# Attention beside a scan and eight experts on one core: values of four score rounds in one step, turned scores first in a round, four exponential buffers

## The reference

```
xn    = layernorm(x)
u     = conv4(xn @ W_in + b_in)               # causal, per channel, 512 channels
h_t   = tanh(A) h_{t-1} + u_t Bp ; y_t = Cp h_t + Dp u_t      # 16 states, 512 steps
out1  = silu(y) @ W_out + b_out
q,k,v = xn @ W_qkv + b_qkv                    # 16 heads of 16
out2  = softmax(q k^T / 4) v
gate  = softmax(xn @ W_gate + b_gate), the best 2 of 8 kept
out3  = sum_e gate_e (xn @ W_experts[e] + b_experts[e])
out   = x + out1 + out2 + out3
```

## Time and profile before

| | |
|---|---|
| median of three runs | 803.84 us |
| the profiled execution itself | 803.87 us |
| its span, first to last instruction | 802.1 us |
| PE busy | 769.0 us (96%) |
| DVE busy | 586.1 us (73%) |
| ACT busy | 535.7 us (67%) |
| POOL busy | 392.5 us (49%) |
| exponentials | 256, 1.03 us each |
| mean granted TensorE clock | 0.992 |

### The profile page before, as it was taken

The page is one execution under the profiler, slowest core; times in us unless marked ns, Lnnn a source line. Parts: engine busy times, 40 slices in busy tenths (PEclk is TensorE's granted clock), DMA queues, the critical chain, the costliest instruction groups (busy, mean ns, idle before and its releaser), DMA issues.

```text
span 802.1 us, 13231 instructions
## 1 busy us (share of the span) xinstructions
PE 769.0 (96%) x4404; PEld 449.3 (56%) x4404; DVE 586.1 (73%) x845; ACT 535.7 (67%) x926; POOL 392.5 (49%) x527
## 2 busy tenths in 40 slices
PE   9789999999999999999999999999999998999996
PEld 7556565665556555565555655555555554554553
DVE  6789966977588676896679775887758877578720
ACT  4647766676676676776667766767666766667774
POOL 7644653574364534563436733355243552425554
PEclk9889999999999999999999999999999999999999
DMA  8302111031110311112111321103111211212000
GB/s 272 66 2 65 44 28 38 18 93 40 41 41 6 90 41 41 41 38 71 40 33 36 83 52 41 41 6 90 40 42 40 54 49 24 52 42 64 19 2 26
DMA packets 32465, 39.09 MB, mean 49 GB/s; under 512 B 8513, under 2 KB 18535, under 8 KB 32398
## 3 DMA queue, kind: packets, MB, share of 16 engines
q1 hardware_dynamic: 31418, 37.29, 17.8%
q10 hardware_dynamic: 852, 0.80, 0.3%
q0 software_dynamic: 128, 0.16, 0.1%
HBM read 8.74 MB, written 4.19 MB: 16 GB/s over the span
## 4 chain that ended last, share of the span: by engine, by line
PE 75%; DVE 18%; issue 4%; ACT 2%; SPq 0%; DMA 0%; POOL 0%; POOLq 0%; DVEq 0%; ACTq 0%
PE PS L456 38%; PE SB L583 12%; DVE mx L1041 10%; PE PS L616 9%; PE TB L600 5%; PE PS L513 4%; DVE ys L891 2%; PE PS L472 2%; PE PS L623 1%; DVE xn L1017 1%; DVE xl L923 1%; PE PS L547 1%; DVE ys L887 1%; PE PS L468 1%; PE PS L526 1%
## 5 line engine op out<-in xcount | busy, mean ns | idle before, releaser
L1041 DVE TENSOR_REDUCE mx<-SB 128x2 f32<-128x1024 f32 x256 | 313.0, 1223 | 153.9 <-PE SB L583 152.9
L1104 POOL TENSOR_TENSOR acc<-acc,mt 128x256 f32<-128x256 f32 x320 | 250.5, 789 | 255.4 <-ACT mt L668 190.0
L823 ACT ACTIVATE Pt<-TB 128x1024 f32<-128x1024 f32 x251 | 257.4, 1026 | 44.0 <-PE TB L600 41.2
L668 ACT ACTIVATE mt<-PS,cpad 128x256 f32<-128x256 f32 x256 | 107.4, 471 | 85.8 <-PE PS L456 85.4
L583 PE MATMUL SB<-kst,qst 48*128 48x512 f32 x512 | 128.6, 499 | 14.9 <-DVE mx L1041 11.5
L616 PE MATMUL PS<-Pt,V 128*17 128x512 f32 x1024 | 134.7, 598 | 1.1 <-ACT Pt L823 1.1
L583 PEld LDWEIGHTS SB<-kst,qst 48*128 48x128 f32 x512 | 47.8, 184 | 117.6 <-DVE mx L1041 63.4
L456 PE MATMUL PS<-weh,xTh 128*128 128x512 f32 x256 | 110.3, 431 | 2.1 <-DVE xl L923 1.1
L600 PE MATMUL TB<-qst,kst 50*128 50x512 f32 x502 | 101.3, 398 | 0.4 <-ACT Pt L823 0.2
L456 PE MATMUL PS<-wel,xTh 128*128 128x512 f32 x256 | 101.3, 396 | 0.0
L456 PE MATMUL PS<-weh,xTl 128*128 128x512 f32 x256 | 100.7, 393 | 0.0
(11 more groups left out here) (162 smaller groups left out, 1158.7 us busy)
## 6 DMA issues: line engine op xcount, KB each, us to landing
qst<-qkh SPq DMA_DIRECT2D x124, 64.0 KB, 2.3
kst<-qkh SPq DMA_DIRECT2D x124, 64.0 KB, 2.3
out<-acc SPq DMA_DIRECT2D x8, 512.0 KB, 2.8
qst<-qkl SPq DMA_DIRECT2D x62, 64.0 KB, 2.2
kst<-qkl SPq DMA_DIRECT2D x62, 64.0 KB, 2.3
acc<-in_x SPq DMA_DIRECT2D x7, 512.0 KB, 3.8
Bt<-in_wexp SPq DMA_DIRECT2D x2, 512.0 KB, 7.9
raw<-in_wexp SPq DMA_DIRECT2D x2, 512.0 KB, 9.6
```

The source lines that it names most:

```text
L668: return e.activation(mt[:, item % NM, :], P, ACT.Copy, scale=scale)
L823: e.activation(Pt[:, T % NP, :, :], turned_bank(T)[:, :, :], ACT.Exp, scale=0.25).then_inc(s_ex, 1)
L1041: e.tensor_reduce(mx[:, g % 2, 0:2, 4 * jj + a], SB[:, :, :], AX.X, ALU.max).then_inc(s_mx, 1)
L1104: e.tensor_tensor(v, v, mt[:, item % NM, :], ALU.add).then_inc(s_mt, 1)
```

## The change

1. `NP = 4`: a fourth buffer of exponentials (4 KB per partition). The DMA scratch of the program is set to 8192 to make room.
2. `values_at(t)`: values are issued in every fourth round, for the exponentials of four rounds at once: in round LAG + 3 + 4m, `values(2m)` and `values(2m+1)`. The second of them reads the exponential of the very round in which it stands.
3. In each round `turned` is written ahead of `score`.
4. The planner puts no unit into a round with values, no Z into the round ahead of one, and has other costs (0.43 for a pair of scores, 0.8 for each values).
5. Four of the eight start-up DMAs go from POOL's queue to ACT's.

```diff
-NP = 3
+NP = 4
...
+def values_at(t):
+
+    m, rest = divmod(t - LAG - 3, 4)
+    return (2 * m, 2 * m + 1) if rest == 0 and 0 <= m < STEPS // 4 else ()
...
-        return 0.45 * pairs + 1.05 * (LAG + 2 <= t < STEPS + LAG + 2 and (t - LAG) % 2 == 0)
+        return 0.43 * pairs + 0.8 * len(values_at(t))
...
-        spent = min(spent, 1.0) + max(left / max(last - t, 1), vector[t]) - fixed(t) - sum(COST[u[0]] for u in row)
+        share = left / max(last - t, 1)
+        spent = min(spent, 1.0) + share + 0.7 * max(vector[t] - share, 0.0) - fixed(t) - sum(COST[u[0]] for u in row)
...
-        while True:
-            k = next((k for k, u in enumerate(todo) if soonest(*u) <= t), None)
-            if k is None or spent < COST[todo[k][0]] / 2 - 0.8 * bare or len(row) > 2 and todo[k][0] != "B":
+        while not values_at(t):
+            k = next((k for k, u in enumerate(todo) if soonest(*u) <= t and not (u[0] == "Z" and values_at(t + 1))), None)
+            if k is None or spent < COST[todo[k][0]] / 2 - 1.2 * bare or len(row) > 2 and todo[k][0] != "B":
...
+                if LAG <= t < STEPS + LAG:
+                    turned(t - LAG)
                 if 0 <= t < STEPS:
                     score(t)
-                if LAG <= t < STEPS + LAG:
-                    turned(t - LAG)
-                m, odd = divmod(t - LAG - 2, 2)
-                if odd == 0 and 0 <= m < STEPS // 2:
+                for m in values_at(t):
                     values(m)
...
-                    else:
+                    elif T < 3:
                         e.wait_ge(s_lo[(W_Q0, W_VG, W_IN)[T]], 1)
...
+                        e.wait_ge(s_kp, 3)
+                        for k in range(4, 8):
+                            shifted_rows(e, k, s_rr[1])
...
-            e.wait_ge(s_kp, 3)
-            for k in range(4, 8):
-                shifted_rows(e, k, s_rr[1])
...
-    nc = _bacc.Bacc("TRN2", target_bir_lowering=False, num_devices=1)
+    nc = _bacc.Bacc("TRN2", target_bir_lowering=False, num_devices=1, dynamic_dma_scratch_size=8192)
```

## The result

The changed kernel takes **841.94 us** (median of 4 runs, 841.14 to 843.75) against 804.07 of the kernel before beside it (803.81 to 805.48): a ratio of 1.047, 95% interval 1.0448 to 1.0492. It is slower by 38 us, where 2.4 us less were forecast; the range ended at 808.5. The profiled execution has a span of 839.3 us, 37.2 more than before.

The account below looks back on a forecast made before the run. PE's own order was taken to bound the kernel (busy 96% of the span), with DVE stopping it in places. Terms -9.9 - 11.9 + 18.4 + 1.0 = -2.4 us took 803.87 to 801.4 us, range 795 to 808.5.

Parts of the forecast that it names:

- Fewer changes of form: On PE, values entered 64 times instead of 128, whole-array work 201 instead of 215: 9.9 us less.
- DVE's stop behind values: Scores right behind values no longer wait on PE for DVE's maximum: 11.9 us less.
- The new wait inside the values: Second values wait on PE for their own round's exponential, 0.37 us behind an M unit: 18.4 us more.
- ACT becomes the bound: Rival: exponentials late in values rounds behind tanh, roundings or copies in ACT's queue, costing 7.6 instead of 1.0: 808; chance 0.18.
- Turned scores first: Turned scores, 0.33 us earlier in their round, sometimes wait on PE for the exponential before: 1.0 us more.
- Start-up DMAs: Four issues moved to ACT cost nothing: PE's 2.67 us idle before the first Z covers 2.69; without cover 2.7 more.
- The fixed rest: Everything else in the kernel: same units, copies and DMAs, larger tile and smaller scratch without an instruction; no time added.
- DVE's lateness moves: Rival: DVE's irregular 4.2 us at scores stay, the later score adds up to 1: about 805; chance 0.12.

Follow-up runs that it names:

- e1: The changed kernel with values one round later and five exponential buffers, the planner following: 800.94 us, ratio 0.9964 to the kernel before.
- e7: e1 with ACT's copy of the values' bank and the unit P that reads it one round later too: 794.83 us, ratio 0.9883.
- e5: The changed kernel with ACT doing the exponential ahead of the previous round's closing unit in values rounds: 824.28 us, ratio 1.0251.
- e2: The changed kernel with score ahead of turned scores in each round again: 840.44 us, ratio 1.0451.
- e4: The kernel before with turned scores ahead of the score in each round, nothing else: 808.60 us, ratio 1.0060.
- e11: The kernel before with the four start-up DMA issues on ACT's queue, nothing else: 806.95 us, ratio 1.0029.
- e6: The changed kernel with a planner that puts at most one Q unit into a round, from round 8 on: 835.60 us, ratio 1.0397.
- e10: The changed kernel with LAG = 12, all one round later in the cycle of eight, the second values' wait kept: 818.41 us, ratio 1.0172.
- e12: e7 with four exponential buffers instead of five: 816.61 us, ratio 1.0148.

## Why the prediction was wrong

Step by step, as the prediction had them:

- *Fewer changes of form*, 9.9 us: right. The ledger has 10.7. Two values follow at 0.87 us, where 0.88 was taken, and not at 0.98: three pairs of the changed kernel and 63 of e1 show it. The rule of the Trainium skill (TensorE: Matmul & The Clock Gate, Part 3, "What overlaps and what doesn't") that weight loads run ahead only onto other rows of the array did not hold here; e1's and e7's pairs show it.
- *DVE's stop behind values*, 11.9 us: right; 11.2 gone.
- *The new wait inside the values*, 18.4 us: the mechanism and its unit price were right (0.83 and 1.91 us against 0.84 and 1.92). The size was low by about 6: eight of 64 pairs are 8.4 us above the price, seven of them since the exponential stood in ACT's queue behind a tanh, most often a late one, and the rest is within 2 us of it. This is what the rival "ACT becomes the bound" had in mind, but it looked for the cost at the turned scores, and it came at the second values. e5 shows what putting the wait right is worth: 17.7 us.
- *Turned scores first*, 1.0 us: right. By the ledger turned scores wait 1.8 us for exponentials in the change and 0.5 before, and e2 took only 1.5 us off by undoing it, which isn't clear of the noise. Alone on the kernel before it costs 4.5 to 5 (e4).
- *Start-up DMAs*, 0: wrong, with the cover misread. PE's 2.67 us of standing before the first Z was the same chain that the issues lengthen, not slack beside it. 2.1 to 2.3 us in e11, within the bound of 2.7. The changed kernel's own trace shows the same 2.1: from SP's first issue to the first Z it takes 14.12 us (25.16 to 39.28) where it took 12.00 (26.04 to 38.04). Its first turned scores are only 0.2 us later than before, since its start-up came to the issues 0.9 us sooner and the rounds behind the first Z took 1.1 us less.
- ***The fixed rest, "the same units, copies and DMAs"*: the step that failed.** The units are the same, but the planner put them in other rounds, and I priced their work and not their waits. 23 us of waits for banks, and 6.5 more in matmuls at the halved clock, whose stretches begin at such waits or right behind them (one at a wait for an exponential), make most of what the prediction lacks; the prediction had no term for the clock. Another 1 to 2 us went to weights not loaded ahead. I had read the order at three places, two around values and one in the start-up. The places that cost most lie at rounds 72 and 104, where the plan's rows read Q, Q and then X, T, T, and at 40, 136 and 168, where they are nearly so. The line of the plan, DVE's five pieces of work between two maxima, and three banks would have shown it: before, the values round 103 with two M stood between Q, Q and X, T, T.

The rival "DVE's lateness moves" had the right engine and 3.6 us for it; it looked for it at the scores, not at the banks.

What stays open: whether 23 us is the price of this phase or of this plan in this phase. e6 changed the plan in the same phase and got 6 us back, e10 changed phase and plan together; a planner that counts DVE's work per round strictly was not tried. That the clock fell because of the waits isn't shown by a run of its own: e7 and e12 have no such stretch between first and last turned scores, e10 and e1 one of 3.4 us, and the changed kernel the three.

## What to carry to other kernels

When a planner moves work, price the waits of what was moved as well as its duration: list, for each unit, which bank it takes, who reads that bank and what stands before that read in the reader's queue; here a move that saved 10 us of changes of form on the busiest engine cost some 30 us in waits for an engine that is 70% busy, and in the halved clock beside them. So compare the row of the granted clock before and after, too. A consumer that takes its data in the very round in which they are made pays whatever stands in the producer's queue, every time; one round and one buffer more turned 841.9 us into 800.9, but 23.5 us of that came with the phase and its plan (e10). Without the buffer it was 816.6 (e12); the buffer without the round was not run. And idle time before a late instruction is slack only for chains that don't end in that instruction.

## What the runs showed of the hardware

Two groups of four float32 matmuls on column strips, with weights on all 128 rows, start 0.870 us apart, 63 times in e7. The second group's first loads show while the first group runs: in one such pair of e7 the groups start at 139.20 and 140.07, and four loads at 139.64. Where the load of a whole-array unit's first weights had waited and started less than 0.06 us ahead of its matmul, the second matmul came 0.09 us later than elsewhere, where loads start 0.11 us ahead or more. That happened some 70 times before and some 80 times in the changed kernel, 6 to 7 us in all, which no list of waits names, since each is shown as "issue". The halved clock of 17.1 us of the changed kernel cost it 6.5 us, which no list of waits names either. Four DMA issues cost ACT 2.58 us (e11) and POOL 2.16 (before).
